# Shared experts' up products of an early-fusion transformer layer: two fp32 products per call become six rounded-format products of split operands

## The reference

```python
def _L0_ffn_ref(x, gate_w, biases, w1, w3, w2, sw1, sw3, sw2):
    xt = x.reshape(B * S, D)                                  # 3088 rows of 128
    shared = silu(xt @ sw1) * (xt @ sw3) @ sw2                # every row
    scores = xt @ gate_w.T
    _, idx = top_k(scores + biases, 2)
    ...                                                       # p: weights of the two
    h = silu(einsum('td,edh->eth', xt, w1)) * einsum('td,edh->eth', xt, w3)
    y = einsum('eth,ehd->etd', h, w2)                         # 8 experts, two are used per row
    return (einsum('te,etd->td', comb, y) + shared)
h = tokens + text
h = h + attention(layernorm(h))
h = h + _L0_ffn_ref(layernorm(h), ...)
```

## Time and profile before

| | us |
|---|---|
| median of three runs | 252.32 (251.96 to 253.23) |
| the profiled execution's own time | 254.19 |
| its span, first to last instruction | 252.3 |
| PE busy | 223.3 (89%) |
| DVE busy | 190.1 (75%) |
| ACT busy | 155.8 (62%) |
| POOL busy | 114.7 (45%) |
| chain that ended last, PE's share | 60% |
| the same, DVE's share | 24% |
| mean granted clock of TensorE | 0.967 |

### The profile page before, as it was taken

How to read it: one execution, slowest core, us unless ns; L and a number is a source line. 1 busy time by engine, 2 the same in 40 slices (tenths; PEclk the granted TensorE clock), 3 DMA queues, 4 the chain that set the end, 5 groups by cost and what they waited for, 6 DMA issues and landing times.

```text
span 252.3 us, 5578 instructions
## 1 busy us (share of the span) xinstructions
PE 223.3 (89%) x1477; PEld 191.5 (76%) x1485; DVE 190.1 (75%) x741; ACT 155.8 (62%) x438; POOL 114.7 (45%) x122
## 2 busy tenths in 40 slices
PE   3888879999899999988989979999999999999930
PEld 2768779989798989766576657888888888887720
DVE  3548896999999999988986778666666666665892
ACT  3056575676876867849863266666666666666390
POOL 1400000084837483803667703666666666666400
PEclk9999995999999999979999999999999999999995
DMA  6999981060607010100113331423332232329666
GB/s 189 353 360 355 328 315 62 0 232 26 233 24 243 22 56 22 42 10 13 55 42 93 79 83 34 115 62 100 92 89 81 84 94 83 90 81 275 159 157 190
DMA packets 31565, 31.68 MB, mean 126 GB/s; under 512 B 4338, under 2 KB 27419, under 8 KB 30768
## 3 DMA queue, kind: packets, MB, share of 16 engines
q1 hardware_dynamic: 27240, 24.57, 32.5%
q0 software_dynamic: 3392, 6.36, 7.7%
q10 hardware_dynamic: 904, 0.41, 0.6%
HBM read 22.80 MB, written 9.03 MB: 126 GB/s over the span
## 4 chain that ended last, share of the span: by engine, by line
PE 60%; DVE 24%; ACT 6%; issue 4%; DMA 2%; SPq 1%; DVEq 0%; ACTq 0%
PE bank L1621 15%; PE bank L1641 10%; PE bank L1630 5%; PE bank L1539 3%; PE bank L1333 3%; PE bank L1524 3%; PE bank L1527 3%; DMA cst<-in_consts 2%; DVE st L842 2%; PE bank L1610 2%; PE bank L1402 2%; PE bank L1416 2%; DVE sh_h L1103 2%; DVE att L908 2%; DVE att L899 2%
## 5 line engine op out<-in xcount | busy, mean ns | idle before, releaser
L813 POOL DMA_INDIRECT xs_dram<-xd,pos_i x50 | 55.4, 1109 | 69.7 <-DVE pos_i L1002 56.9
L824 POOL DMA_INDIRECT y_dram<-att,goal x56 | 55.1, 985 | 37.3 <-ACT att L749 37.0
L1333 PE MATMUL bank<-wt,xp_both 128*128 128x128 f32 x288 | 39.6, 290 | 5.7 <-DMA xp_both<-in_patches 5.4
L1333 PEld LDWEIGHTS bank<-wt,xp_both 128*128 128x128 f32 x288 | 37.3, 202 | 7.3 <-DMA xp_both<-in_patches 5.9
L735 ACT ACTIVATE att<-bank 128x256 f32<-128x256 f32 x56 | 21.5, 384 | 24.4 <-PE bank L1621 24.0
L1240 DVE CAST xsT_h<-bank 128x128 fp32r<-128x128 f32 x56 | 16.3, 291 | 24.4 <-PE bank L1610 24.4
L1641 PE MATMUL bank<-w_sb,att 128*128 x224 | 34.7, 277 | 0.0
L1641 PEld LDWEIGHTS bank<-w_sb,att 128*128 128x128 f32 x224 | 29.4, 191 | 0.5 <-issue 0.2
L1621 PE MATMUL bank<-xp_both,xsT_h 128*128 x56 | 26.8, 479 | 0.8 <-DVE xsT_l L1242 0.8
L1253 DVE TENSOR_TENSOR att<-att,bank 128x256 f32<-128x256 f32 x56 | 23.0, 411 | 1.7 <-ACT att L735 1.7
L1621 PE MATMUL bank<-xp_both,xsT_l 128*128 x56 | 22.2, 396 | 0.0
(11 more groups left out here) (212 smaller groups left out, 498.7 us busy)
## 6 DMA issues: line engine op xcount, KB each, us to landing
xp_both<-in_patches SPq DMA_DIRECT2D x6, 1152.0 KB
xs_all<-xs_dram SPq DMA_DIRECT2D x56, 64.5 KB, 1.8
xd<-y_dram SPq DMA_DIRECT2D x8, 384.0 KB, 4.8
w<-in_w SPq DMA_DIRECT2D x2, 1024.0 KB, 11.3
y_dram<-att,goal POOLq DMA_INDIRECT x56, 2.3
xs_dram<-xd,pos_i POOLq DMA_INDIRECT x50
xp_both<-in_patches SPq DMA_DIRECT2D x1, 768.0 KB, 5.6
hrow<-in_txt SPq DMA_DIRECT2D x2, 384.0 KB, 6.9
```

The source lines that it names most:

```text
L813: nc.gpsimd.indirect_dma_start(out=xs_dram[:, :], out_offset=bass.IndirectOffsetOnAxis(ap=pos_i[0:rows, j, k:k + 1], axis=0), in_=xd[0:row ...
L824: nc.gpsimd.indirect_dma_start(out=y_dram[:, :], out_offset=bass.IndirectOffsetOnAxis(ap=goal[u][:, 0:1].bitcast(I32), axis=0), in_=ys[u][ ...
L1333: M(ps[:, 0:D], xp[p][:, k, :], wt[:, k, :], start=(k == 0), stop=False)
```

## The change

The up products of the shared experts are made as the experts' own are: the rows and the weights are each split into a part rounded to `fp32r` (`x2T_h`, `sw13_h`) and the remainder (`x2T_l`, `sw13_l`), and each fp32 product becomes three `fp32r` products.

- TensorE: each call has six products in the place of two, and waits for the remainders of its group.
- ACT rounds the turned rows of each group (`round_columns`), in the loop after the columns of the next group, and in the tail behind the table load and ahead of the first silu; it rounds the shared weights in iteration 3. The one copy of all class columns (L682) becomes a copy of two columns per group (`keep_class`).
- GpSimd takes the remainder of each group's rows (`remainders`), that of group g+1 behind the scatters of group g, the first ahead of all scatters and the last behind all; the remainder of the weights comes behind the scatters of group 1.
- `x2T` and the sum of attention and centre tap (`s_all`, now `s_two`) keep two groups in place of all, with waits that guard them; two semaphores of DVE (`raw_done`, `slots_done`) go.

```diff
+            def round_columns(g):
+                n = 3 * P + (B if g == G - 1 else 0)
+                act.wait_ge(x2T_done, 2 * g + 1)
+                nc.scalar.copy(x2T_h[:, 3 * P * g:3 * P * g + n], x2T[g % 2][:, 0:n]).then_inc(x2T_done, 1)
...
             def columns2(g):
                 act.wait_ge(x2_turned, g + 1)
-                nc.scalar.copy(x2T[:, 3 * P * g:3 * P * g + 3 * P], bank[6][:, 0:3 * P]).then_inc(x2T_done, 1)
+                after(act, xl_done, XL[g - 2] if g > 1 else 0)
+                after(act, gate_done, g - 1)
+                nc.scalar.copy(x2T[g % 2][:, 0:3 * P], bank[6][:, 0:3 * P]).then_inc(x2T_done, 1)
...
                 columns1(i + 1)
+                round_columns(i - 1)
+                if i == 3:
+                    act.wait_ge(s_wexp, 96)
+                    nc.scalar.copy(sw13_h[:], sw13[:]).then_inc(wh_done, 1)
                 if i == G - 2:
                     centre_tap(G - 1)
+                keep_class(i - 1)
                 inverse_log(i)
...
             act.preload_act_table(ACT.Silu)
+            round_columns(G - 2)
+            keep_class(G - 2)
             shared_silu(0, 0)
             scores(G - 2)
-            act.wait_ge(s_done, G)
-            nc.scalar.copy(s_col[:].rearrange("p (g b) -> p g b", b=2), s_all[:, :, 0:2]).then_inc(s_done, 1)
+            keep_class(G - 1)
...
+            def remainders(g):
+                n = 3 * P + (B if g == G - 1 else 0)
+                at = slice(3 * P * g, 3 * P * g + n)
+                pool.wait_ge(x2T_done, 2 * g + 2)
+                nc.gpsimd.tensor_tensor(x2T_l[:, at], x2T[g % 2][:, 0:n], x2T_h[:, at].bitcast(F32), ALU.subtract
+                                        ).then_inc(xl_done, 1)
+            remainders(0)
             for g in range(G):
                 ...                                  # the scatters of group g
+                if g == 1:
+                    remainders(2)
+                    pool.wait_ge(wh_done, 1)
+                    nc.gpsimd.tensor_tensor(sw13_l[:], sw13[:], sw13_h[:].bitcast(F32), ALU.subtract).then_inc(xl_done, 1)
+                elif g < G - 2:
+                    remainders(g + 1)
+                elif g == G - 1:
+                    remainders(G - 1)
...
             def mixed(g):
-                V.tensor_tensor(s_all[:, g, :], ot[:], hl[g % 2][:], ALU.add).then_inc(s_done, 1)
+                after(dve, kept, g - 1)
+                V.tensor_tensor(s_two[g % 2][:], ot[:], hl[g % 2][:], ALU.add).then_inc(s_done, 1)
...
             def shared_up(c, m):
-                x = x2T[:, at:at + n]
-                M(bank[second][:, 0:n], sw13[:, HID + P * m:HID + P * m + P], x, start=True, stop=True)
-                if c == 0 and m == 1:
-                    pe.wait_ge(qc_done, G)
-                M(bank[first][:, 0:n], sw13[:, P * m:P * m + P], x, start=True, stop=True).then_inc(sh_up, 1)
+                pe.wait_ge(xl_done, XL[max(min(c, G - 1), 3)])
+                x_h, x_l = x2T_h[:, at:at + n], x2T_l[:, at:at + n]
+                for part, ps in ((HID + P * m, bank[second]), (P * m, bank[first])):
+                    if c == 0 and m == 1 and part < HID:
+                        pe.wait_ge(qc_done, G)
+                    for i, (w, x) in enumerate(((sw13_h, x_h), (sw13_h, x_l), (sw13_l, x_h))):
+                        last = M(ps[:, 0:n], w[:, part:part + P], x, start=(i == 0), stop=(i == 2))
+                last.then_inc(sh_up, 1)
```

More of the change, by code:

```diff
@@ L139, in build @@
         sw13 = sb("sw13", [P, 2 * HID])
+        sw13_h = sb("sw13_h", [P, 2 * HID], F32R)
+        sw13_l = sb("sw13_l", [P, 2 * HID], F32R)
         sw2_sb = sb("sw2_sb", [P, 2, D])
@@ L155, in build @@
         ex, ft, cc, ss, rr = (att[:, i, :, :] for i in range(5))
+        bq_part, bq_sel = att[0:4, 0, 0:2, :], att[0:4, 1, 0:2, :]
+        bq_h = att[0:4, 2].rearrange("p t c -> p (t c)")[:, 0:3 * D].bitcast(BF16).rearrange("p (k c) -> p k c", k=3)
         qq = sb("qq", [P, 2, SEQ, 2])
@@ L163, in build @@
         hl = [sb(f"hl{i}", [P, 2 * SEQ]) for i in range(2)]
-        s_all = sb("s_all", [P, G, 2 * SEQ])
+        s_two = [sb(f"s_two{i}", [P, 2 * SEQ]) for i in range(2)]
         s_col = sb("s_col", [P, B])
-        x2T = sb("x2T", [P, J * P])
+        x2T = [sb(f"x2T{i}", [P, 3 * P + B]) for i in range(2)]
+        x2T_h, x2T_l = (sb(f"x2T_{k}", [P, CLS * P + B], F32R) for k in "hl")
         xcls = sb("xcls", [B, D])
@@ L259, in build @@
         both_done, place_done, pr_done, pos_done = (sem(n) for n in ("both_done", "place_done", "pr_done", "pos_done"))
[L260 removed]
+        xl_done, twice_done = sem("xl_done"), sem("twice_done")
         scattered, padded, tab_done, ends_done = sem("scattered"), sem("padded"), sem("tab_done"), sem("ends_done")
         cols_done, cols_turned = sem("cols_done"), sem("cols_turned")
[L263 removed]
+        top_done, sg_done, weight_done, kept = sem("top_done"), sem("sg_done"), sem("weight_done"), sem("kept")
         sh_up, sh_act, sh_mul, sh_down, sh_add = (
@@ L305, in build @@
         SH = G + 1
+        XL = [g + 1 if g < 3 else g + 2 for g in range(G)]
         EARLY = 6
@@ L482, in scores, with keep_class @@
                     "p (j e) -> p j e", e=E)).then_inc(sc_done, 1)
+            def keep_class(g):
+                act.wait_ge(s_done, g + 1)
+                nc.scalar.copy(s_col[:, 2 * g:2 * g + 2], s_two[g % 2][:, 0:2]).then_inc(kept, 1)
             def exps_most(g):
@@ L705, in _ @@
             act.wait_ge(x2_turned, G)
-            nc.scalar.copy(x2T[:, 3 * P * (G - 1):3 * P * (G - 1) + 3 * P + B], bank[6][:, 0:3 * P + B]).then_inc(x2T_done, 1)
+            act.wait_ge(xl_done, XL[G - 3])
+            act.wait_ge(gate_done, G - 2)
+            nc.scalar.copy(x2T[(G - 1) % 2][:], bank[6][:, 0:3 * P + B]).then_inc(x2T_done, 1)
+            round_columns(G - 1)
             round_w13(5)
@@ L958, in raw_best @@
                 for j in tiles_of(g):
-                    V.max(raw8[:, j, :], sc[:, j, :]).then_inc(raw_done, 1)
+                    V.max(raw8[:, j, :], sc[:, j, :])
             def choices(g):
@@ L997, in positions @@
                 dve.wait_ge(pr_done, g + 1)
-                V.tensor_reduce(pos_2[:, a:b, :], prod[:, a:b], AX.X, ALU.add).then_inc(slots_done, 1)
-                dve.wait_ge(slots_done, g + 1)
+                then(V.tensor_reduce(pos_2[:, a:b, :], prod[:, a:b], AX.X, ALU.add))
                 with nc.allow_low_precision(reason="whole numbers below 2 ** 24"):
@@ L1114, in remainder_w13 @@
             def remainder_w13(e):
-                dve.wait_ge(wh_done, e + 1)
+                dve.wait_ge(wh_done, e + 2)
                 part = slice(e * 2 * HID, (e + 1) * 2 * HID)
@@ L1363, in mixed_rows @@
                 pe.wait_ge(qrc_done, g + 1)
-                T(bank[3][:, 0:P], s_all[:, g, 2:2 + P], ident)
+                T(bank[3][:, 0:P], s_two[g % 2][:, 2:2 + P], ident)
                 for b in range(2):
-                    last = T(bank[3][:, P * (1 + b):P * (2 + b)], text_cols(s_all[:, g, :], 2 + P, b), ident)
+                    last = T(bank[3][:, P * (1 + b):P * (2 + b)], text_cols(s_two[g % 2], 2 + P, b), ident)
                 last.then_inc(sr_done, 1)
             def mixed_cls():
-                pe.wait_ge(s_done, G + 1)
+                pe.wait_ge(kept, G)
                 pe.wait_ge(h2_done, G)
@@ L1432, in gate @@
             def gate(g):
-                pe.wait_ge(x2T_done, g + 1)
+                pe.wait_ge(x2T_done, 2 * g + 1)
                 for t, j in enumerate(tiles_of(g)):
                     rows = rows_of(j)
-                    last = M(bank[6][0:rows, GATE_AT + E * t:GATE_AT + E * t + E], x2T[:, P * j:P * j + rows], gate_sb,
+                    last = M(bank[6][0:rows, GATE_AT + E * t:GATE_AT + E * t + E], x2T[g % 2][:, P * t:P * t + rows], gate_sb,
                              start=True, stop=True)
```

4 lines of the change are left out of this document (removed).

## The result

The changed kernel takes 260.59 us (median of four runs, 257.9 to 262.54) against 252.6 before: a ratio of 1.0281, 95% interval 1.0193 to 1.0369. Forecast was 250.9, a gain; it is a loss of 7.1 us by the ratio and 8.0 by the medians, and the profiled execution (261.12, span 259.3) shows where.

The account below looks back on a forecast made before the run. TensorE's expert loop was taken to move as a block, its start set by the TensorE and DVE chain before it. Terms -1.3 - 0.25 + 0.1 = -1.45 on the median 252.32 gave 250.9; forecast 250.4 to 251.5, range 250.0 to 253.2.

Parts of the forecast that it names:

- the one on GpSimd: GpSimd's subtractions between scatters: they fit into its waits for positions, so nothing is late; cost put at nothing.
- DVE held by GpSimd: Rival, tail: the last subtraction excludes DVE's remainder of expert 7's weights; up to 0.86 lost, 251.7; chance 0.09.
- The size of a subtraction: GpSimd, 384 columns: taken as 0.86 us, or 1.7 if a second input costs as much as the first.
- The clock rival: Start of the expert loop: TensorE idles about 1.1 us and the clock falls; costs about 1, 251.9; chance 0.06.
- The products: TensorE's up calls: three fp32r products take 0.53 per half in place of 0.66, saving 0.125 per half.
- the wait behind the loop: DVE's wait of 1.26 for TensorE behind the expert loop becomes 1.0, as call (7, 0) saves 0.25.
- The last shared product: Tail, on DVE: it comes at about 146.2 in place of 147.54, 1.3 earlier.
- The cap on the start: Start of the expert loop: row tiles allow the first product at about 148.8, so the gain is 1.3 at most.
- The 1.3 that TensorE gains: Tail: 11 halves by 0.125 give 1.35, less 0.05 for ACT, so TensorE and DVE reach the expert loop earlier.
- The term that I put at nothing: Tail: the scatters' end, which the row tiles' loading follows, moves by less than 0.3 either way; counted as nothing.
- ACT in the loop: Rounding and copy, 0.45 to 0.5 per group, covered by idle time, cost nothing; rival 252.7 to 255.1, chance 0.17.

Follow-up runs that it names:

- the roundings alone: The kernel before with ACT's roundings into spare buffers that nobody reads, fp32 products kept and no subtractions: 254.07 us, ratio 1.0027.
- the nearest with the full arithmetic: Changed kernel, subtractions moved (group 6's to DVE), group 6's rounding behind the third silu pair, ten unread products ahead of the expert loop: 252.86 us, ratio 1.0004.

## Why the prediction was wrong

- The step that failed is the one on GpSimd: "Subtraction 6 falls into the 2.30 us in which GpSimd waits for positions and fits at either bound", and "In the loop GpSimd waits for positions ahead of every group, so nothing there is late". I asked only whether GpSimd had time, which it had, not what DVE does in it. What the runs showed in its place: the subtractions hold DVE, which my sum has at nothing; without them the time is 6.0 us less (5.4 by the ratios). Moving them took 5.5 us off, together with ACT's rounding of group 6.
- The rival with the right mechanism, DVE held by GpSimd, had a chance of 0.09, one place (the last subtraction) and 0.86 as its price. The last subtraction did hold DVE there (1.63 in place of 0.68), at no cost that reaches the start of the expert loop; the loss came from five other places, 6.5 us of DVE's time. The rule named beside it, in the Trainium skill ("SBUF — State Buffer", "Who interferes with whom"), is what the traces show: reads by GpSimd against DVE operations with two inputs in SBUF, whole operations long (0.56 became 3.02 beside 1.01 and 1.27). Every subtraction should have been laid beside DVE's row, with the two that follow each other first, since these hold DVE for both.
- The size of a subtraction was 1.02 for 384 columns, between my 0.86 and the bound of 1.7.
- The clock rival (0.06, "costs about 1") came true at the start of the expert loop: without subtractions filling the wait took 2.4 us off the median, 1.15 of it shown in that stage. I had read that the clock stayed at 1.00 behind waits of 0.64 and 0.75, and had named 1.1 as the wait to come; it was 1.32 and 0.89. In the tail the same happened behind DVE's hold, which I had not considered.
- The products were right: 0.53 per half, 1.06 per call, the wait behind the loop shorter by 0.24 against 0.25. The last shared product came 1.1 earlier without subtractions (forecast 1.3).
- The cap on the start was misjudged. I had both ways agree at 148.8, with scatters that move by less than 0.3. They ended 0.8 to 1.5 later, measured from the last sum, in every profiled version of the change without a held sum, and since the row tiles are loaded behind them, the start stayed 31.1 to 32.2 behind that sum, against 31.3. The 1.3 that TensorE gains becomes a wait for the tiles. The term that I put at nothing was the way of the scatters: the rounding ahead of the first silu moves them (0.3 with the roundings alone), and transfers that start just behind DVE's remainder take up to 0.5 longer.
- ACT in the loop was right as far as the stage tells: 74.03 without subtractions against 73.84.

No version beats the kernel before beyond its interval; the nearest with the full arithmetic has ratio 1.0004.

## What to carry to other kernels

An engine that is idle is not free: before work goes to GpSimd, look at what DVE does in the same moments, and count a read there as time of DVE wherever DVE has both inputs in SBUF, and look the other way too, at what DVE does when GpSimd starts a transfer; a wait on DVE's own semaphore can put it beside operations that read a bank. A faster TensorE ahead of a wait for data gains nothing, and when its idle time grows the clock can take back what was saved (1.15 against 1.1 here); look at every gap that a saving makes longer.

## What the runs showed of the hardware

- A subtraction of 384 columns on GpSimd takes 1.02 with two different inputs, 0.83 with the same input twice, a copy 0.52, filling 640 columns 0.65.
- Reads of SBUF by GpSimd and DVE operations with two inputs there exclude each other (0.56 became 0.89 to 3.02); writes don't (0.56 and 0.63 side by side). The recorded starts don't tell which of the two waits: a sum that started 0.36 ahead of a subtraction was held, and so was a step of 0.2 that started 0.62 ahead of one, while a sum that started 0.03 ahead of a copy was not.
- A transfer of a full row tile that GpSimd starts 0.06 to 0.37 behind the start of such a DVE operation (128x512, 0.67 to 0.72) takes 1.15 to 1.46 in place of 0.97; seen in every profile, tested by no run.
- Ten products that nobody reads, 1.75 us of work, ahead of the expert loop took 2.4 us off the median without subtractions; the granted clock stayed at 1.00 there, where it had been 0.50.
- Executions of the unchanged kernel spread from 250.6 to 257.3 us over the study; the mean granted clock of executions of one kernel differs (0.967 to 0.988 for the roundings alone). In the profile of that kernel's quickest execution the clock doesn't fall near 110 us, and the loop's stage is 72.94.
